# Expert weights of the splat attention read as f32 in the loop, without a bf16 copy in device memory

## What is computed

```python
def _L0_attn_ref(x, ..., splat_positions, ..., We, be, Wt, bt, Wd, bd, Wg, bg):
    std_out = softmax(q k^T / 8) v                              # 16 heads of 64
    infl = exp(-0.5 * d2 / scales^2) * |importance|             # (b, n, 64)
    gathered = einsum('bns,bnd->bsd', infl, x) / total
    enc = relu(gathered @ We + be)                              # (b, 64, 512)
    trans = einsum('bsd,sde->bse', enc, Wt) + bt                # Wt: (64, 512, 512), f32
    dec = trans @ Wd + bd
    flow = einsum('bns,bsd->bnd', infl, dec) * sigmoid(x @ Wg + bg)
    return (0.6 * std_out + 0.4 * flow) @ Wo

x = x + 0.5 * _L0_ffn_ref(layernorm(x))     # mixture of 8 experts, top 2
x = x + _L0_attn_ref(layernorm(x))
x = x + 0.5 * _L0_ffn_ref(layernorm(x))
x = x + 0.5 * _L1_ffn_ref(layernorm(x))     # light and heavy feed-forward
x = x + _L1_attn_ref(layernorm(x))          # gated scan
x = x + 0.5 * _L1_ffn_ref(layernorm(x))
```

## Time and profile before

| what | us |
|---|---|
| three runs, median | 12356.49 |
| three runs, lowest and highest | 12058.42 and 12403.93 |
| the profiled execution, its own time | 11979.58 |
| the span of its slowest core (core 7), first to last instruction | 11978.1 |
| the spans of the eight cores | 11946.7 to 11978.1 |
| mean granted TensorE clock of the eight cores | 0.797 to 0.802 |

### The profile page before, as it was taken

How to read it: one execution, slowest core, us unless ns; L and a number is a source line. 1 busy time by engine, 2 the same in 40 slices (tenths; PEclk the granted TensorE clock), 3 DMA queues, 4 the chain that set the end, 5 groups by cost and what they waited for, 6 DMA issues and landing times.

```text
span 11978.1 us, 105005 instructions; the slowest of 8 cores (11946.7 to 11978.1 us)
## 1 busy us (share of the span) xinstructions
PE 8316.9 (69%) x33181; PEld 3274.9 (27%) x33181; DVE 3785.9 (32%) x7756; ACT 2583.9 (22%) x4375; POOL 1216.0 (10%) x2127
## 2 busy tenths in 40 slices
PE   1019867777789459763696977777769838965488
PEld 1004322222234223221232422222224313321133
DVE  1014414444444320124202432444444431023310
ACT  0000113444410111221111021444430111132111
POOL 1200010000000004100131001000000002400033
PEclk6559878888889569885797978888889858976599
DMA  7971041001000014200143014001001002400034
GB/s 145 101 92 43 15 131 11 6 6 8 8 32 29 13 37 129 65 18 13 51 131 117 36 34 104 6 6 8 6 9 43 25 3 91 127 22 22 1 107 142
DMA packets 383398, 595.11 MB, mean 50 GB/s; under 512 B 215092, under 2 KB 266484, under 8 KB 376216
## 3 DMA queue, kind: packets, MB, share of 16 engines
q0 software_dynamic: 356400, 533.38, 20.0%
q1 hardware_dynamic: 26472, 55.02, 1.5%
HBM read 663.94 MB, written 88.21 MB: 63 GB/s over the span
## 4 chain that ended last, share of the span: by engine, by line
PE 56%; DVE 16%; DMA 9%; issue 8%; ACT 5%; another core or an unknown queue 4%; DVEq 1%; POOL 1%; ACTq 0%; SPq 0%; POOLq 0%; PEld 0%; PEldq 0%
PE ps L645 7%; PE ps L647 7%; PE ps L1510 7%; PE ps L997 5%; DMA LNXP<-w2hp_scr 4%; DVE DPOOL L1031 4%; PE ps L1530 3%; PE ps L1088 3%; PE ps L1113 2%; PE ps L1607 2%; ACT SCR L532 2%; PE ps L1276 2%; PE ps L1291 2%; PE ps L665 2%
## 5 line engine op out<-in xcount | busy, mean ns | idle before, releaser
L1095 ACT ACTIVATE SCR<-ps,NEGM 128x512 bf16<-128x512 f32 x2048 | 1258.5, 702 | 1540.3 <-PE ps L1088 1535.2
L645 PE MATMUL ps<-SCRB,LNXT 128*128 128x512 bf16 x4096 | 1557.1, 380 | 0.0
L647 PE MATMUL ps<-SCRB,LNXT 128*128 128x512 bf16 x4096 | 1556.5, 380 | 0.0
L1530 PE MATMUL ps<-LNXP,SCRB 128*128 128x512 bf16 x4096 | 987.6, 383 | 141.3 <-DMA LNXP<-w2hp_scr 99.3
L1088 PE MATMUL ps<-INFL 128*128 128x512 bf16 x2048 | 881.7, 452 | 55.3 <-ACT SCR L1095 51.3
L1113 PE MATMUL ps<-SCR,LNXP 128*65 128x512 bf16 x2048 | 879.4, 437 | 44.4 <-ACT SCR L1095 42.1
L1510 PE MATMUL ps<-LNXT,LNXP 128*128 128x512 bf16 x4096 | 890.9, 379 | 11.4 <-DMA LNXP<-w1pk_scr 11.3
L532 ACT ACTIVATE SCR<-X 128x1024 bf16<-128x1024 f32 x192 | 203.1, 1058 | 3160.6 <-DVEq L98 2269.3
L1516 ACT ACTIVATE SCRB<-ps,B1HC 128x512 bf16<-128x512 f32 x512 | 353.0, 689 | 1871.2 <-PE ps L1510 1871.2
L653 DVE SCALAR_TENSOR_TENSOR X<-ps,G,X 128x512 f32<-128x512 f32 x512 | 384.7, 751 | 1058.1 <-PE ps L647 1058.1
L1541 DVE SCALAR_TENSOR_TENSOR X<-ps,MASK,X 128x512 f32<-128x512 f32 x128 | 87.2, 745 | 1979.3 <-PE ps L1538 1979.3
(11 more groups left out here) (361 smaller groups left out, 8076.9 us busy)
## 6 DMA issues: line engine op xcount, KB each, us to landing
LNXP<-w1pk_scr POOLq DMA_DIRECT2D x512, 256.0 KB, 2.9
LNXP<-w2hp_scr POOLq DMA_DIRECT2D x1024, 128.0 KB, 2.4
SCRB<-wet_scr POOLq DMA_DIRECT2D x32, 2048.0 KB, 8.1
LNXP<-wtb_scr POOLq DMA_DIRECT2D x128, 512.0 KB, 4.5
wtb_scr<-L_attn_Wt POOLq DMA_DIRECT2D x64, 512.0 KB, 119.6
X<-L_attn_x SPq DMA_DIRECT2D x8, 2048.0 KB, 23.7
SCRB<-L_ffn_We POOLq DMA_DIRECT2D x32, 512.0 KB, 18.4
wet_scr<-SCRB SPq DMA_DIRECT2D x16, 1024.0 KB, 7.9
```

Source lines behind the costliest of these rows:

```text
L645: E["t"].matmul(b_.ps[bk0][:], LNXT[:, icx, ts(t)], we[:, icx, 0:512], start=(icx == 0), stop=(icx == IC - 1))
L647: mm = E["t"].matmul(b_.ps[bk1][:], LNXT[:, icx, ts(t)], we[:, icx, 512:1024], start=(icx == 0), stop=(icx == IC - 1))
L1095: tk_e = b_.sig("s", E["s"].activation(out=ATTS[j % 4], in_=b_.ps[SCB[j % 3]][:], func=AF.Exp, scale=0.0625, bias=A["NEGM"][:, 0:1]))
L1530: mm = E["t"].matmul(bank[:], HHT[:, hc, ts(tt)], W2BF[:, sl, 0:512], start=(hc == 0), stop=False)
```

## The change

The scratch tensor `wtb_scr`, the 64 DMAs of the prologue that fill it, and their semaphores go. `wt_load` reads the f32 matrix straight from the input and turns it into bf16 on the way into the slot. Slots, order, the number of loads in the loop (64 for each sequence) and all arithmetic stay as they are.

```diff
-                 "ha", "hb", "hg", "hh", "pw1", "pw2", "pp2", "pp3", "pp4", "pst2",
-                 "pw3", "pw4", "pw5", "pw6", "pw7", "pw8", "pw9", "pw10"]
+                 "ha", "hb", "hg", "hh", "pw1", "pw2", "pp2", "pp3", "pp4", "pst2"]
...
-    ORDERED = {"ppst", "pw3", "pw4"}
+    ORDERED = {"ppst"}
...
-    wtb_h = nc.dram_tensor("wtb_scr", [64, 128, 2048], BF16, kind="Internal").ap()
...
-        tk_wtb = [None] * 8
-        for s in range(64):
-            tk_wtb[s // 8] = b_.dma("g", wtb_h[s].rearrange("p (ec f) -> p ec f", ec=4),
-                                    H["L0_attn_Wt"][s].rearrange("(ec p) f -> p ec f", p=128),
-                                    sem=f"pw{3 + s // 8}")
...
     def wt_load(s):
         sl = s % 4
         b_.wait("g", tk_used[sl])
-        b_.wait("g", tk_wtb[s // 8])
         tk_wt[sl] = b_.dma("g", WT4[:, sl, :, :],
-                           wtb_h[s].rearrange("p (ec f) -> p ec f", ec=4), sem=wt_sems[sl])
+                           H["L0_attn_Wt"][s].rearrange("(ec p) f -> p ec f", p=128),
+                           sem=wt_sems[sl])
```

More of the change, by code:

```diff
@@ L485, in build @@
                         IDB, rms=False)
-                emit_l0attn(b_, nc, H, X, LNX, LNXP, LNXT, SCRB, A, IDB, ONESR, trd_h, wtb_h, tk_wtb)
+                emit_l0attn(b_, nc, H, X, LNX, LNXP, LNXT, SCRB, A, IDB, ONESR, trd_h)
                 n_done = 2
@@ L671, in emit_moe, with emit_l0attn @@
     b_.barrier()
-def emit_l0attn(b_, nc, H, X, LNX, LNXP, LNXT, SCRB, A, IDB, ONESR, trd_h, wtb_h, tk_wtb):
+def emit_l0attn(b_, nc, H, X, LNX, LNXP, LNXT, SCRB, A, IDB, ONESR, trd_h):
     E = b_.e
```

## The result

| what | before | after |
|---|---|---|
| timed runs, median (lowest to highest) | 12245.1 (11993.5 to 12456.8), 10 runs | 12016.5 (11786.7 to 12342.3), 9 runs |
| ratio of the runs, 95% interval | | 0.979 (0.976 to 0.983) |
| the profiled execution, its own time | 11979.6 | 11794.6 |
| the spans of its eight cores | 11946.7 to 11978.1 | 11749.8 to 11793.2 |

The change makes the kernel 1.5 to 2.1% faster: 185 us on the two profiled executions, a ratio of 0.979 on the runs. The interval ends on both sides of 2%, so whether the gain is over 2% stays open here.

The account below looks back on a forecast made before the run. The prologue was taken as DMA-bound, gate-unit turns as TensorE-bound, other turns by nothing alone. Removing copies gives -300 us, slower f32 loads +120: -180, 11,800 us profiled, 11,880 predicted on the lowest run; range 11,760 to 12,240.

Parts of the forecast that it names:

- within 2%: Whole kernel: the measured time differs from the unchanged kernel by at most 2%; chance 0.85.
- first half of `Wg`: Loop: this load, queued behind five slower matrix loads, lands at 1588.1 us instead of 1578.8, +9.3 us.
- 16 turns with a gate unit: Loop: loads of 3.4 us lag turns of 3.1 by 4.5 us, less than the 9 us lead, so 0 us.
- second half of `Wg`: Loop: it waits for a 1.8 us longer load ahead and the 4.5 us lag, +6 us on 9.6.
- from its landing to the last splat matmul's end: Loop after the second half of `Wg`: 43 remaining loads at 3.4 us make 153.9 us, +44.3.
- The second way: Prologue: 64 copies write 33.6 MB, which at 108 GB/s is 311 us saved.
- transfer time D: Loops: one f32 matrix load takes 3.4 us of all 16 DMA engines, between 3.07 and 3.54.
- in between: Rival, loops: a long stream is slower, D 3.7 to 4.7 us, gain only 10 to 140 us; chance 0.14.
- The cover of four slots: Loop, turns with gate units: three loads of lead (9 us) hide the slower loads, lost with D above 3.7.
- The loads stay at the rate of the prologue's copies, 108 GB/s: Rival, loops: D is 4.85 to 5.3 us, total +10 to +72 us, so not faster; chance 0.06.
- The loads hide better: Rival, loops: never-empty queue at 171 GB/s, +24 us a sequence, -252 us in all; chance 0.07.
- the prologue keeps its wait: Rival, prologue: something else is late too, so only the loops' 120 us loss remains, 12,100; chance 0.03.

Follow-up runs that it names:

- e9: The changed kernel once more, beside the kernel before on one chip: ratio of the runs 0.982, -203 us (0.983) on cores that kept their clock.
- e2: Kernel before without the 64 prologue copies, loops reading bf16 from `wet_scr` (other numbers): -297 us on cores that kept their clock.
- e1: Kernel before with its 64 copies kept, only the loops reading f32 input: 12070.5 us against 11964.6 on highest-clock cores, partly from a lower clock.
- e5: Kernel before with the 64 copies moved behind the first mixture stage's matmuls, loops reading bf16: -321 us on cores that kept their clock.
- e7: Changed kernel with the 32 gate units spread, one in each second turn: 11767.7 us in one group of cores that kept their clock, -219 against before.
- e6: Kernel before with all 128 prologue copies moved into the first sequence's two mixture stages: 11504.2 us, -483, on cores that kept their clock.

## Why the prediction was right

The sum was -300 + 120 = -180 us, 11,800 us on the profiled basis; the profiled execution has 11794.6, and the undisturbed cores of e9 have -203. Both terms erred to the same side: the prologue gave 301 to 318 us, not 300, and the two loops cost 104 to 113 us, not 120. The range 11,760 to 12,240 holds the median of the runs, 12016.5, but that says little: its upper end is only 5 us under the median of the unchanged kernel (12245.1). What bears the prediction out are the sum and the steps. The single value of 11,880 was the sum on the lowest run then shown, 12058.4; the lowest runs of the kernel before are at 11,969 to 11,997 in the four comparisons, those of the changed one at 11,787 and 11,754. It is therefore some 90 to 130 us too high for such a run. Of "within 2%", to which I gave 0.85, the runs say nothing firm: both intervals of the ratio, 0.976 to 0.983 and 0.977 to 0.987, hold 0.98, and the undisturbed cores stand at 0.983.

Step by step, on core 7 and for the first sequence, whose loop grew most of the eight; that the whole loop agrees to 0.2 us is in part luck:

| step | predicted | measured |
|---|---|---|
| landing of `L1_attn_xp_w` | 782.3 to 482, -300 | 464.2, -318 (-301 to -305 on cores 0, 3, 5) |
| first half of `Wg`, from the first issue | +9.3 | 17.0 to 24.5, +7.5 |
| 16 turns with a gate unit | 0 | 52.1 to 53.8, +1.7 |
| second half of `Wg` | +6 | 9.6 to 16.3, +6.7 |
| from its landing to the last splat matmul's end | 109.6 to 153.9, +44.3 | 109.6 to 153.5, +43.9 |
| one loop | +60 | +59.8 |

- **The prologue.** The mechanism was right, and e2 shows it alone. The size was short by 18 us on core 7. I took the last copy into `w2hp_scr` to land at 480, as it had in the trace of before, 83.3 us after its issue; without copies behind it, it needs 69.1 us and lands at 463.5. That the copies behind it had slowed it shows in the other runs: the longest of the last two or three is 79 to 83 us on cores 5 and 7 in the two kernels that have these copies (the kernel before, and e1, whose core 7 is shown below), and 63 to 73 us on the same cores in the seven that have none behind it (the changed kernel, e2 to e5, e7 and e9). On core 0 it is 76 and 80 against 64 to 76, and on core 3 there is no difference. The other 4 us are an issue 2.3 us sooner and a shorter step from there to the small load. The second way, bytes by rate, gave 311.

```profile
L67 POOL DMA_DIRECT2D w2hp_scr<-L_ffn_w_heavy x2: 893/894/896, 396.4 to 396.9; - x2
...
DMA to landing us min/median/max: 68.5/74.7/80.9
```

- **The transfer time D.** I took 3.4 us between 3.07 and 3.54, from short bursts. The 43 loads bear it out, and so do the windows, 156 GB/s in the turns without a gate unit (0.524 / 156 = 3.4). A loop-long stream on eight cores stays within the rates of the bursts, 148 to 173 GB/s, though at their slow end: e7 has 148 over 217 us, D = 3.5. The rival "in between" needed D from 3.7 on, and it falls.
- **The cover of four slots.** It held with D = 3.4 against turns of 3.1 us: TensorE is busy for all of 50 us in the second window with gate units. The loss comes where TensorE has no other work, as predicted.
- **The loads stay at the rate of the prologue's copies, 108 GB/s.** It falls. e1 has both in one kernel and on one core: its copies run at 108 GB/s in this window, its loads of the same f32 rows at 158 in the window shown with e1. The copies read no more than the loads; what they have besides is that they write to device memory. No run varies that alone.

```profile
500.00:700.00 200.00, 0.00 (x0) 0.00 (x0) 0.00 (x0) 0.00 (x0) 24.93 (x35) 0.50 1.02 108
```

- **The loads hide better, and the prologue keeps its wait.** The first would need loops 24 us longer; they are 50 to 60 longer. Its picture was close all the same: over the whole first loop of core 7, in the window below, the engines have a mean share of 1.01, and e7 shows that their bytes bind the loop. What was wrong is the rate, 171 GB/s where the loop has 145. The second falls with `L1_attn_xp_w`; but e6 shows its wait, 10 us for `CONVW`, once the other copies are gone.

```profile
1243.00:1491.00 248.00, 160.91 (x544) 45.61 (x544) 21.32 (x32) 39.22 (x65) 49.23 (x66) 0.72 1.01 145
```

- **What the profile would show.** The granted clock falls to 0.56 in the turns without a gate unit, where it was 0.91, and four splat matmuls take 1.86 us, not 1.02. My sign of being wrong was a clock that falls there and stays low behind the loop; only its first half has come. In these turns the loads bind anyway, and behind the loop the clock is as it was: the windows of 50 and then 100 us behind the last splat matmul, on core 7, first of the kernel before and then of the changed one, show this.

```profile
1750.00:1800.00 50.00, 31.60 (x77) 8.23 (x76) 27.15 (x41) 0.00 (x0) 2.23 (x3) 0.59 0.26 44
1800.00:1900.00 100.00, 75.46 (x305) 30.36 (x303) 35.97 (x63) 0.37 (x1) 7.89 (x9) 0.86 0.23 21
```

```profile
1491.00:1541.00 50.00, 32.21 (x79) 8.26 (x79) 25.76 (x41) 0.00 (x0) 2.22 (x3) 0.55 0.26 44
1541.00:1641.00 100.00, 74.85 (x303) 30.09 (x301) 35.97 (x63) 1.75 (x2) 7.87 (x9) 0.87 0.24 21
```

The wait of the splat matmuls for their loads, for which I gave 70 us, is 53.1 in the first loop of core 7, by its waits from 1240 to 1500 us:

```profile
PE ps L845 <- DMA LNXP<-L_attn_Wt: 53.1, 32, 6.2
```

The matmuls at the lower clock make up the difference: in the 32 turns TensorE is busy for 55.1 us, where it was 36.4 us, so that 19 us of what I had counted as waiting are work.

## What to carry to other kernels

A conversion of weights that is done once pays only if it costs less than it saves: here 64 copies cost 300 us in a prologue where nothing else ran, and saved 50 to 60 us in each of two loops. The better question was where they run: behind the mixture stage's matmuls, where the DMA share had been 0.09, they cost nothing that the spans show and keep the fast loops (-321 us against -203). To price a load in a new form, take the rate of a load of the same form in the trace at a DMA share of 1 (here between 148 and 173 GB/s, which left 80 to 135 us for the loops), then count the loads that remain once every slot is full.

## What was not expected of the hardware

- Reading bf16 in pieces of 1 KB costs little against 4 KB (loops of 186 to 195 us against 182 to 190). f32 turned into bf16 runs at 156 to 158 GB/s written on core 7 in pieces of 1 KB, and at 167 in pieces of 4 KB.
- Copies queued behind a DMA can make it land later, though it was issued first: 81 to 83 us against 63 to 73 on core 7 (the kernel before and e1 against the seven without copies behind it), 79 against 63 to 70 on core 5, and nothing on core 3.
- The DMA engines write 114 GB/s of copies and expert weights under a full TensorE, and its waits in that window name no load of expert weights (e6).
